# Around the seam between attention and experts: the last quad's sums behind the routing, first relus between its powers, its outputs between expert units

## The reference

```python
# block 1: attention by inverse squared distance, 16 heads of 64
P = X @ W_in + b_in                       # per head: Q, K, V, G
W = (EPS + cdist(Q, K)) ** -2             # sqrt, log, exp on the chip
W = W / (EPS + W.sum(-1, keepdims=True))
H = G * (W @ V)
x = x + H @ W_out + b_out
# block 2: 8 experts, the best 2 of each token
route = softmax(xn @ Wr + br); keep the 2 largest, divide by their sum
h = relu(xn @ W1[e] + b1[e])              # 128 -> 512
y = h @ W2[e] + b2[e]                     # 512 -> 128
x = x + sum_e routed[e] * y[e]
# block 3: linear attention; block 4: top 384 of 512 tokens get gelu(x @ w_block)
```

## Time and profile before

| | |
|---|---|
| median of 3 runs | 1485.12 us (1484.88 to 1485.7) |
| profiled execution | 1486.39 us, its span 1484.6 us |
| busy: TensorE, weight loads, VectorE, ScalarE, GpSimd | 96%, 47%, 69%, 70%, 47% |
| mean granted clock of TensorE | 0.979 of full |
| first half, until the last `av` product | about 961 us |

### The profile page before, as it was taken

How to read it: one execution, slowest core, us unless ns; L and a number is a source line. 1 busy time by engine, 2 the same in 40 slices (tenths; PEclk the granted TensorE clock), 3 DMA queues, 4 the chain that set the end, 5 groups by cost and what they waited for, 6 DMA issues and landing times.

```text
span 1484.6 us, 17096 instructions
## 1 busy us (share of the span) xinstructions
PE 1423.0 (96%) x6192; PEld 699.3 (47%) x6192; DVE 1022.3 (69%) x1928; ACT 1036.0 (70%) x831; POOL 702.8 (47%) x555
## 2 busy tenths in 40 slices
PE   6999999999999999999999999699999999999974
PEld 3433433434433433433443443256666666666643
DVE  6786777777777777777787776744567576575564
ACT  2799789789879978978978979644555454554531
POOL 4568767777777777678768768600000000000000
PEclk9999999999999999999999999799999999999985
DMA  3001111010011001002001003332101011010100
GB/s 112 0 16 23 29 30 23 15 44 23 16 37 30 16 19 48 16 16 51 16 16 38 22 16 102 80 137 87 46 20 64 1 65 58 8 65 15 50 8 8
DMA packets 45845, 55.08 MB, mean 37 GB/s; under 512 B 13824, under 2 KB 32512, under 8 KB 44608
## 3 DMA queue, kind: packets, MB, share of 16 engines
q1 hardware_dynamic: 45760, 53.97, 12.2%
HBM read 49.11 MB, written 4.85 MB: 36 GB/s over the span
## 4 chain that ended last, share of the span: by engine, by line
PE 89%; DVE 7%; POOL 1%; ACT 1%; issue 1%; DMA 1%; SPq 0%; DVEq 0%; POOLq 0%
PE sc L383 15%; PE y L1076 14%; PE av L396 14%; PE pj L74 12%; PE z L74 12%; PE sc L378 5%; PE pj L362 4%; PE pj L412 4%; PE pj L404 2%; DVE w L541 2%; PE tb L1012 1%; POOL wsum L303 1%; PE tb L1026 1%; PE tb L1039 1%; DMA bout<-in_b_out 1%
## 5 line engine op out<-in xcount | busy, mean ns | idle before, releaser
L541 DVE TENSOR_SCALAR w<-sc 128x1024 f32<-128x1024 f32 x256 | 301.5, 1219 | 117.1 <-PE sc L383 116.0
L914 ACT ACTIVATE hr<-z,b 128x512 f32<-128x512 f32 x256 | 175.8, 687 | 239.4 <-PE z L74 239.2
L303 POOL TENSOR_TENSOR wsum<-wsum,w 128x512 f32<-128x512 f32 x256 | 329.3, 1286 | 20.1
L632 ACT ACTIVATE w<-w 128x2048 f32<-128x2048 f32 x128 | 237.7, 1906 | 144.4 <-DVE w L541 144.0
L1076 PE MATMUL y<-hr,w 128*128 128x512 f32 x512 | 261.4, 593 | 0.0
L383 PE MATMUL sc<-query,key 64*128 64x512 f32 x1024 | 254.4, 615 | 0.0
L396 PE MATMUL av<-w,vt 128*64 128x512 f32 x1024 | 237.7, 607 | 6.2 <-DVE gT L548 5.4
L636 ACT ACTIVATE w<-w 128x2048 f32<-128x2048 f32 x128 | 240.5, 1903 | 0.4
L640 ACT ACTIVATE w<-w 128x2048 f32<-128x2048 f32 x128 | 239.9, 1899 | 0.0
L74 PE MATMUL z<-xs_h,w_h 128*128 128x512 f32 x256 | 201.3, 786 | 0.1
L289 POOL TENSOR_TENSOR sqq<-query 128x512 f32<-128x512 f32 x64 | 66.7, 1041 | 224.0 <-DVE query L495 221.9
(11 more groups left out here) (173 smaller groups left out, 1909.7 us busy)
## 6 DMA issues: line engine op xcount, KB each, us to landing
hT<-head_recips SPq DMA_DIRECT2D x64, 256.0 KB, 4.0
rb<-routing SPq DMA_DIRECT2D x8, 2048.0 KB, 7.3
w<-in_W SPq DMA_DIRECT2D x16, 256.0 KB, 4.9
xa<-in_X SPq DMA_DIRECT2D x8, 256.0 KB, 4.4
xc<-in_X SPq DMA_DIRECT2D x8, 256.0 KB, 2.8
x<-xc SPq DMA_DIRECT2D x8, 256.0 KB, 4.0
out<-prod SPq DMA_DIRECT2D x8, 256.0 KB, 2.3
x<-x SPq DMA_DIRECT2D x1, 1792.0 KB, 11.5
```

The source lines that it names most:

```text
L303: nc.gpsimd.tensor_tensor(wsum[:, u, :], wsum[:, u, :], w[:, j % 2, u, c, :], ALU.add).then_inc(s_added, 1)
L541: nc.vector.tensor_scalar(w[:, s, 2 * r:2 * r + 2, c, :], sc[:, i, :, :], 0.0, None, ALU.max).then_inc(s_d2, 1)
L632: nc.scalar.activation(w[:, j % 2, u, :, :], w[:, j % 2, u, :, :], ACT.Sqrt).then_inc(s_sqrt, 1)
L914: nc.scalar.activation(hr[:, n % HR, :], z[:, n % 2, :], ACT.Relu, bias=b1[:, n % NU:n % NU + 1]).then_inc(S["hr"], 1)
```

## The change

Each engine's list between the halves, and what stands at which unit of batch 0, is written in another order. In the diff: GpSimd holds the last quad's sums until the routing of batch 0 is done (`S["rw"]`) and puts the normalization of quad 30 between them; ScalarE takes two logarithms and then two powers, and puts the first six relus between the rest; TensorE does two hidden products before the first `av` product of the last quad and has the second one, quad 30's output, quad 31's sums and output and the turn of batch 7's output at later units; VectorE follows with the same.

```diff
@@ gpsimd
+            normalize(NQ - 3)
+            pool.wait_ge(S["rw"], 1)
+            add_chunks(NQ - 1, 0)
+            add_chunks(NQ - 1, 1)
+            normalize(NQ - 2)
+            add_chunks(NQ - 1, 2)
+            add_chunks(NQ - 1, 3)
+            normalize(NQ - 1)
@@ scalar, between the halves
             logarithm(NQ - 1, 0)
-            for u in range(4):
-                if u < 3:
-                    logarithm(NQ - 1, u + 1)
-                if u == 3:
-                    exponential(0)
-                power(NQ - 1, u)
+            logarithm(NQ - 1, 1)
+            power(NQ - 1, 0)
+            power(NQ - 1, 1)
+            exponential(0)
+            logarithm(NQ - 1, 2)
             act.wait_ge(S["in_front"], 16 * len(front_loads))
+            hidden(0)
+            hidden(1)
+            power(NQ - 1, 2)
+            hidden(2)
+            hidden(3)
+            logarithm(NQ - 1, 3)
+            hidden(4)
+            power(NQ - 1, 3)
+            hidden(5)
+            turned_routing(0)
@@ tensor, step(b, k)
-                if (b, k) == (0, 0):
+                if (b, k) == (0, 1):
+                    turn_routing(0)
+                if (b, k) == (0, 2):
+                    weighted_values(NQ - 1, 1)
+                if (b, k) == (0, 6):
+                    output(NQ - 2)
+                if (b, k) == (0, 10):
                     sums(NQ - 1)
-                if (b, k) == (0, 2):
-                    output(NQ - 2)
-                if (b, k) == (0, 14):
+                if (b, k) == (0, 20):
                     output(NQ - 1)
-                if (b, k) == (0, 16):
+                if (b, k) == (0, 22):
                     turn_output(B - 1)
@@ tensor, between the halves
+            turn_f(0)
             pe.wait_ge(S["in_front"], 16 * len(front_loads))
-            turn_f(0)
             logits(0)
-            weighted_values(NQ - 1, 0)
-            weighted_values(NQ - 1, 1)
             for n in range(AHEAD):
                 if n == 2:
-                    turn_routing(0)
+                    weighted_values(NQ - 1, 0)
                 hidden(n)
@@ vector, step(b, k)
-                if (b, k) == (0, 5):
+                if (b, k) == (0, 4):
+                    weighted_values(NQ - 1, 1)
+                    for e in range(5, NE):
+                        split_w1(e)
+                if (b, k) == (0, 8):
+                    output(NQ - 2)
+                    dve.wait_ge(S["in_b2"], 16)
+                if (b, k) == (0, 12):
                     sums(NQ - 1)
-                if (b, k) == (0, 6):
-                    output(NQ - 2)
-                if (b, k) == (0, 8):
-                    dve.wait_ge(S["in_b2"], 16)
-                    dve.wait_ge(att["added"], 12 * NQ)
-                if (b, k) == (0, 9):
+                if (b, k) == (0, 18):
                     reciprocals(NQ - 1)
-                if (b, k) == (0, 19):
+                if (b, k) == (0, 27):
                     output(NQ - 1)
-                if (b, k) == (0, 21):
+                if (b, k) == (0, 29):
                     add_output(B - 1)
@@ vector, between the halves
+            dve.wait_ge(att["added"], 12 * (NQ - 1))
+            front_norm(0)
             sums(NQ - 2)
             output(NQ - 3)
-            dve.wait_ge(att["added"], 12 * (NQ - 1))
-            front_norm(0)
-            split_w1(0)
             dve.wait_ge(S["turn_f"], 1)
...
             hand_over(0)
+            split_w1(0)
             softmax_start(0)
-            reciprocals(NQ - 2)
-            for e in range(1, 4):
-                split_w1(e)
-            weighted_values(NQ - 1, 0)
+            split_w1(1)
             softmax_end(0)
             expert_ranks(0)
             routing(0)
-            for e in range(4, NE):
-                split_w1(e)
-            weighted_values(NQ - 1, 1)
+            weighted_values(NQ - 1, 0)
+            split_w1(2)
+            reciprocals(NQ - 2)
+            split_w1(3)
+            split_w1(4)
```

More of the change, by code:

```diff
@@ L214, in build_attention @@
                     use[name] = len(use)
+        use["out", NQ - 2], use["sum", NQ - 1] = sorted((use["out", NQ - 2], use["sum", NQ - 1]))
         def weights_to_split():
@@ L310, in normalize @@
                                         gT[:, 2 * q:2 * q + 2, :], ALU.mult).then_inc(s_hT, 1)
-            for j in PERIODS:
+            for j in range(-1, NQ):
                 if 0 <= j - 3 < NQ:
@@ L324, in gpsimd @@
                         add_chunks(j - 1, u)
+            return add_chunks, normalize
         def tensor(pe):
@@ L869, in _ @@
         def _(pool):
-            att_gpsimd(pool)
+            add_chunks, normalize = att_gpsimd(pool)
+            normalize(NQ - 3)
[6 more added lines that the diff above has]
+            normalize(NQ - 1)
             pool.wait_ge(att["x1_out"], 16 * B)
@@ L933, in step @@
                         root_t(t, 1)
-                if (b, k) == (0, 2):
-                    turned_routing(0)
                 if f < B:
@@ L944, in step @@
                         turned_routing(f)
-                if b < B:
+                if b < B and b * NU + k >= AHEAD:
                     hidden(b * NU + k)
             square_roots, logarithm, power = att_scalar(act)
+            root_f(0)
             square_roots(NQ - 1)
-            root_f(0)
             nc.scalar.preload_act_table_set("natural_log_exp_and_others")
             logarithm(NQ - 1, 0)
-            for u in range(4):
-                if u < 3:
-                    logarithm(NQ - 1, u + 1)
-                if u == 3:
-                    exponential(0)
-                power(NQ - 1, u)
-            act.wait_ge(S["in_front"], 16 * len(front_loads))
+            logarithm(NQ - 1, 1)
[3 more added lines that the diff above has]
+            logarithm(NQ - 1, 2)
+            act.wait_ge(S["in_front"], 16 * len(front_loads))
+            hidden(0)
[8 more added lines that the diff above has]
+            turned_routing(0)
             for b in range(B + 2):
```

## The result

The changed kernel takes 1484.05 us (median of 20 runs, 1480.9 to 1486.98), the kernel before in the same sessions 1485.77 (20 runs, 1484.59 to 1488.95). The ratio is 0.9985, with an interval of 0.9978 to 0.9992: 1 to 3 us faster, just under what I had called the least that can be told, and 1.3 us above the forecast. The profiled execution took 1482.43 us, with a span of 1480.6. The runs further on come from two later sessions: e1, e3, e4 and e5, where the kernel before took 1486.04 us, and e6, e7, e8 and e10, where it took 1485.94, with one stray execution of 3608 us left out.

A forecast was written before the change was run, and what follows sets the result against it. TensorE, busy 96% of the span, was taken as the bound, with only idle time and low clock between the halves to win. Front −9.2, constants' wait +5.2 and low clock +1.7 gave −2.3 us: 1482.8 us, range 1477.5 to 1488.5.

The forecast's parts named there:

- The front: From the end of quad 30's second product to unit 14 with batch 1's turn: 9.2 us won, between 7.5 and 10.5.
- 4.5 us at low clock behind the restart of unit 0: TensorE's hidden units 0 and 1: clock taken as low for 4.5 us, first product of quad 31 ending at 949.0.
- waits of 0.9, 0.4 and 0.3 us: TensorE waits: 0.9 us for relu 4, 0.4 more for relu 5, 0.3 at unit 8 for VectorE's first weighing.
- The bet that a gap of this size leaves the clock high: TensorE gaps of 0.9 and 0.4 us assumed to leave the clock high; if lost for 3.4 us, 1.7 us go.
- The premise: TensorE is busy 96% of the span, so only its idle time and its low clock, both between the halves, can pay.
- The wait for the constants: Hidden unit 34 waits 5.2 us for relu 32, which waits for the tail's constants, landing at 1022.5.
- The low clock behind it: TensorE at low clock behind the gap at hidden unit 34: costs 1.7 us, up to 3.4.
- The sum: Whole kernel: −9.2 + 5.2 + 1.7 = −2.3 us, giving 1482.8 us.
- 1475.9: Rival, 12 in 100: the tail's constants are not waited for, so the front's 9.2 us stand alone.
- The load of the batches: Rival, 15 in 100: it lands late, hidden unit 19 waits 2.7 us plus 3.0 of low clock; 1488.5 us.
- The lock's rival: Rival, 5 in 100: VectorE's three splits beside GpSimd take 1.9 us longer, holding first weighing and unit 8; 1484.7 us.

The follow-up runs named there:

- e1: The changed kernel with all three engines' waits for the tail's constants moved from batch 1's start to their first readers: 1476.4 us, ratio to before 0.9932.
- e3: The kernel before with the same three waits for the tail's constants moved to their first readers: 1485.75 us, ratio 0.9999.
- e4: The kernel before with only quad 31's output, its turn and batch 7's addition moved to later units: 1494.98 us, ratio 1.0055.
- e5: The changed kernel without GpSimd's wait for the routing ahead of quad 31's sums: 1486.02 us, ratio to before 0.9998.
- e6: e1 with ScalarE's first six relus behind the last power, as in the kernel before: 1479.9 us, ratio to before 0.9962.
- e7: The changed kernel with only ScalarE's wait for the tail's constants moved, to before unit 17 of batch 1: 1476.63 us, ratio to before 0.994.
- e8: e1 with VectorE's normalization and split of expert 0's weights behind quad 30's sums and quad 29's output again: 1480.2 us, ratio to before 0.9961.
- e10: The changed kernel with SyncE's eleven constant loads ahead of the store of batch 7's attention output, waits unmoved: 1477.51 us, ratio to before 0.994.

## Why the prediction was right, and where its sizes were off

*The front, 9.2 forecast, 10.0 in the profile* (9.6 by the medians of e1 and before, 9.3 and 8.4 by those of e7 and e10). The steps came as written. The turn ran from 936.98 where I had 938.0, which is 8.4 us behind F0 for a forecast of 8.7; the logits waited 1.03 us for the copy; unit 0 waited for two short pairs of splits and started 12.3 us behind F0 (forecast 12.4). The first product of quad 31 followed without a wait (943.70). Two sizes differ. I took 4.5 us at low clock behind the restart of unit 0; it was 2.8, and in e7 none: that is the 0.8 us (the product ends 18.8 us behind F0, forecast 19.7). And I booked waits of 0.9, 0.4 and 0.3 us behind relus 4 and 5 and the weighing, where there was one of 0.56; but from the product's end to unit 14 I needed 33.1 us (949.0 to 982.1) and the profile 33.2. The missing microsecond lies between the two products of quad 31, 8.0 us for my 7.7: beside the one wait, the hidden products and expert units took 7.5 us for my 6.4. The chain there is ScalarE's, as the view of what ended last has it for the kernel after:

```profile
949.66 1.80 ACT w L639
...
952.04 1.80 ACT w L643
```

So the logarithm and the power between the relus did hold TensorE, as I had it, in smaller pieces. The bet that a gap of this size leaves the clock high held, in the profile of after and in e1. That the front came so near its forecast is in part luck: the profiles with this front have won 9.3 to 12.1 us (52.7 to 49.9 for 62.0), and the 12.1 of e7 lies outside my bounds of 7.5 and 10.5, by a clock that I had taken as low.

*The premise.* I started from two things that can pay, idle time and low clock. In the order before, the second hardly did behind quad 29's output: e4 shows that time saved there by TensorE is waited away, since the chain is VectorE's. In the changed order it does pay: e7 and after have the same order up to unit 14 and differ by 2.1 us of front, in the output and in hidden units 0 and 1, which ran at the higher clock in e7.

*Who won it.* Undoing one part at a time costs 2.0 us (hold), 3.5 (relus) and 3.8 (place of the normalization and the first split) by the medians, 3.7, 2.5 and 2.4 by the fronts of the profiles. Each of the three wins something. But their sums, 9.3 and 8.6, don't divide the 10 us among them: in e5, e6 and e8 quad 31's second product starts without idle time, so none of them brings back the 5.4 us gap of the earlier trace rows, the largest piece. Two parts of the change bear on it and were not undone: VectorE gates the first product ahead of the splits of experts 2 to 4 (in the kernel before it stood behind those of 1 to 3, until 954.49), and TensorE has hidden and expert units between the two products. Which of them is enough is open. The expectations of e6 and e8 were too small by more than half against the medians: I priced the idle time of TensorE and not the low clock that follows it. In e6 that is 1.6 us, in e8 1.25 in the product; e8's median lies where I had put the rival (1478.5 or more), and the profile accounts for 2.4 of its 3.8 us.

*The wait for the constants, 5.2 forecast, 5.21 measured in the profile of after* (4.90 in e5). The chain from the addition to the last landing was forecast at 11.9 us (1010.6 to 1022.5) and was 12.0. e4 produced this wait without the rest of the change, e3 showed that the wait costs nothing in its old place, and e7 that ScalarE's is the one that counts.

*The low clock behind it, 1.7 forecast, 1.5 measured*, by the stretches 1012.40 to 1015.50; 2.75 in e4.

*The sum, −2.3 forecast, −1.7 measured by the medians.* The profiled executions differ by 4.0: 0.7 of that is F0, ahead of the change, and 3.3 is the change, −10.0 + 6.7. The ratio's interval, 1 to 3 us, holds both −2.3 and −1.7. The profile's 3.3 is at its edge. The front's clock differs from one execution to the next (e1, e7, e10); that this is part of the 6 us over which the 20 runs spread (4.4 for the kernel before) is likely and not shown.

*The rivals.* The constants were waited for, so 1475.9 did not come; e1 and e7, in which they are not waited for, took 1476.4 and 1476.6, the time that this rival had. The load of the batches came in time: GpSimd was done at 969.1 (forecast 970), the load was issued at 969.16 and took 7.8 us alone, for 11.5 in the earlier trace rows and 7 taken. So it landed at 977.0. VectorE's rows show how close that was:

```profile
975.85 0.69 DVE L1330 TENSOR_TENSOR yT<-yT,ye 128x512 f32<-128x512 f32 x1
977.01 0.29 DVE L675 BATCH_NORM_STATS2 stats_f<-x 128x6 f32<-128x128 f32 x1 [0.47 <-issue]
```

The statistics start with the landing, 0.47 us after the operation ahead; the profile puts this down to the issue, and that it was the load is inferred from the two times. Nothing on TensorE waited for it. I had put the point from which the load decides at 979, 49.7 us behind F0; it landed 48.4 us behind it, so the rival was missed by 1.3 us. The lock's rival did not come either: splits beside GpSimd took 3.1 us a pair, as in the earlier trace rows.

## What to carry to other kernels

A wait at the head of a loop for data that is first read much later costs nothing until some work is moved behind which the data's loads are queued; then it costs its full length. When work is moved later, follow the queue behind it to the last load and look for every engine that waits for it, and put such waits at the first reader. Cut two profiles at events that both have, and add up the pieces: here one piece was equal to 0.1 us in all seven kernels without the wait and showed the give-back exactly, while the total moved by more than the effect from one execution to the next. And before you price an engine's low clock or idle time, look whether the chain runs over it there. Undoing the parts of a change one by one shows which of them win something, and not how the whole is divided among them.

## What was new about the hardware

*One and the same gap may cost clock at once, later or not at all.* After the 2.6 us gap before the sums of quad 30 the granted clock was low at once in the earlier trace rows (the sums took 1.94 us), in e7 and in e10 (1.93), and in the profile of after only from the output on (so in e1, e3, e6 and e8), as these two stretches show:

```profile
931.17:933.50 2.33, 1.06 (x8) 0.18 (x9) 2.29 (x3) 2.31 (x2) 2.18 (x1) 1.00 1.13 335
933.50:936.90 3.40, 3.40 (x4) 1.37 (x5) 1.30 (x4) 3.39 (x3) 0.00 (x0) 0.50 0.72 163
```

The sums ran at full clock (1.06 us for 1.94), the output at half. In e4 both ran at full clock (1.07 and 1.95 us), and so did the product behind the gap of 2.5 us at 952.44. So behind gaps of 2.5 and 2.6 us the low clock cost between nothing and some 3 us (6.1 us at 0.50 in the earlier trace rows), behind those of 4.3 and 5.2 us 2.75 and 1.5; gaps of 0.56 us cost none. The Trainium skill (TensorE: Matmul & The Clock Gate, "What's actually happening") says that the hardware that grants the clock is not reset when a kernel starts, and that the point of the change varies by 500 ns either way for that reason. That is said of the first rise in a kernel; for the fall behind a gap the traces agree that the point varies for one order and one gap, but by more: by at least the 1.06 us of the sums, and in e4 it did not fall.

*Short VectorE operations can be held too.* Once in the profile of after a subtraction of 32 elements in each partition, which took 0.19 us at 941.08, stood beside GpSimd's product:

```profile
987.11 2.30 DVE L1197 TENSOR_TENSOR lg<-lg,m 128x32 f32<-128x32 f32 x1
```

```profile
987.00 2.37 POOL L311 TENSOR_TENSOR hT<-hT,gT 128x1024 f32<-128x1024 f32 x1 [17.87 <-DMA hT<-head_recips]
```

It ended 0.04 us behind the product's end. The Trainium skill (SBUF — State Buffer, "Who interferes with whom") says that an operation of VectorE with two inputs in SBUF contends with a GpSimd instruction that reads SBUF, and calls the port pair that they share an exclusive lock. The row agrees, with 2.30 us for 0.19, to the end of GpSimd's instruction, and in e5 the same operation took 0.83 us beside GpSimd's sums (at 944.70). Nothing waited for it here, but the reason to hold GpSimd until a routing is done is the same: the normalization of four 128x128 pieces took 2.93 us beside GpSimd (931.27) and 1.12 alone (in e8, at 940.32), hidden only because TensorE had work.
